# A graph network on one core: edge lists loaded as 128 equal rows, and the first layer's features scaled and split in two parts on two engines ahead of the barrier

## The reference

```python
def _L0_gnn_ref(label, src, dst):
    out_deg = jnp.clip(jax.ops.segment_sum(ones, src, num_segments=n), 1.0)
    in_deg = jnp.clip(jax.ops.segment_sum(ones, dst, num_segments=n), 1.0)
    h = label * (out_deg ** (-0.5))[:, None]
    agg = jax.ops.segment_sum(h[src], dst, num_segments=n)
    return agg * (in_deg ** (-0.5))[:, None]
...
h = jnp.maximum(_layernorm(x, axis=-1), 0.0)
x = x + _L0_gnn_ref(h, src, dst)
h = jnp.maximum(_layernorm(x, axis=-1), 0.0)
x = x + _L1_gnn_ref(h, edge_index, ...)      # two attention layers
h = jnp.maximum(_layernorm(x, axis=-1), 0.0)
x = x + _L2_gnn_ref(h, edge_index, ...)      # attention, rows normalized
h = jnp.maximum(_layernorm(x, axis=-1), 0.0)
x = x + _L3_gnn_ref(h, edge_index, edge_weight1, ...)   # message passing, log_softmax
```

## Time and profile before

| what | value |
|---|---|
| median of 3 runs | 4518.12 us (4517.07 to 4518.27) |
| the profiled execution | 4518.98 us |
| its span | 4516.9 us |
| TensorE busy | 3870.6 us (86%) |
| VectorE busy | 3402.5 us (75%) |
| ScalarE busy | 2879.3 us (64%) |
| GpSimd busy | 516.7 us (11%) |
| mean granted TensorE clock | 0.958 of full speed |

### The profile page before, as it was taken

The page is one execution under the profiler, slowest core; times in us unless marked ns, Lnnn a source line. Parts: engine busy times, 40 slices in busy tenths (PEclk is TensorE's granted clock), DMA queues, the critical chain, the costliest instruction groups (busy, mean ns, idle before and its releaser), DMA issues.

```text
span 4516.9 us, 64954 instructions
## 1 busy us (share of the span) xinstructions
PE 3870.6 (86%) x19132; PEld 2004.2 (44%) x19133; DVE 3402.5 (75%) x5028; ACT 2879.3 (64%) x3229; POOL 516.7 (11%) x1356
## 2 busy tenths in 40 slices
PE   0549999999983998999699999987999998999998
PEld 0546666667651333333333333332333332555555
DVE  4999889889866999996699999879998987211101
ACT  1117677677753999999499999967999997000001
POOL 0005555555510000000000000000000000000000
PEclk9989999999986999999899999998999999999998
DMA  1004344334447454543255444324454541977776
GB/s 45 23 1 149 126 136 156 134 122 155 141 173 93 154 167 151 163 157 114 83 186 165 159 149 160 119 79 157 150 171 151 173 139 54 279 218 239 240 234 188
DMA packets 624622, 660.79 MB, mean 146 GB/s; under 512 B 147489, under 2 KB 590115, under 8 KB 616996
## 3 DMA queue, kind: packets, MB, share of 16 engines
q1 hardware_dynamic: 603898, 524.06, 38.9%
q10 hardware_dynamic: 20524, 134.07, 7.3%
...
## 4 chain that ended last, share of the span: by engine, by line
PE 17%; issue 14%; DVE 8%; DVEq 8%; ACT 5%; DMA 0%; ACTq 0%; SPq 0%
PE psum L1945 12%; DVE sb_arena L1432 5%; ACT sb_arena L2310 4%; DVEq L1435 4%; DVEq L1395 3%; PE psum L1900 2%; DVE sb_arena L1397 2%; ACT psum L2302 1%; PE psum L1991 0%; PE psum L1911 0%; PE psum L1990 0%; DVE sb_arena L1525 0%; PE psum L1974 0%; PE psum L1972 0%; PE psum L1962 0%
## 5 line engine op out<-in xcount | busy, mean ns | idle before, releaser
L1900 PE MATMUL psum<-sb_arena 128*65 128x448 f32 x4116 | 1729.4, 542 | 190.0 <-DVE sb_arena L1432 177.6
L1432 DVE SCALAR_TENSOR_TENSOR sb_arena<-sb_arena 128x896 f32<-128x896 f32 x1029 | 1071.4, 1088 | 206.7 <-ACT sb_arena L2310 189.7
L2302 ACT ACTIVATE psum<-sb_arena,sb_sj 128x896 f32 (+1 forms) x1029 | 1041.0, 1012 | 219.3 <-PE psum L1878 95.9
L2310 ACT ACTIVATE sb_arena<-psum,sb_sj 128x896 f32<-128x896 f32 x1029 | 1019.7, 991 | 96.9 <-PE psum L1911 96.5
L1397 DVE CUSTOM_DVE_ANT_0 sb_arena<-sb_arena 128x6272 uint8<-128x6272 uint8 (+2 forms) x189 | 990.5, 5240 | 74.0 <-DMA sb_arena<-linked 32.7
L1900 PEld LDWEIGHTS psum<-sb_arena 128*65 128x65 f32 x4116 | 557.0, 138 | 881.9 <-issue 501.4
L950 DVE TENSOR_SCALAR sb_arena<-sb_arena 128x392 f16<-128x392 f16 x2352 | 651.1, 344 | 0.0
L1911 PE MATMUL psum<-sb_arena,sb_ones 128*128 128x448 bf16 x2058 | 567.0, 358 | 45.8 <-ACT sb_arena L2279 25.0
L1945 PE MATMUL psum<-sb_arena 128*128 128x448 f16 (+1 forms) x2744 | 544.7, 359 | 33.3 <-DVE sb_arena L1525 22.5
L1687 PE MATMUL psum<-sb_arena 128*128 128x392 f16 x2352 | 476.6, 339 | 38.7 <-DVE sb_arena L950 28.8
L2127 ACT ACTIVATE sb_arena<-psum 128x784 f16<-128x784 f32 x392 | 322.8, 823 | 281.8 <-PE psum L1687 278.7
...
## 6 DMA issues: line engine op xcount, KB each, us to landing
sb_arena<-counts SPq DMA_DIRECT2D x490, 784.0 KB, 6.4
...
sb_arena<-records SPq DMA_DIRECT2D x784, 6.0 KB, 1.7
...
```

The costliest lines, as they stand in the source:

```text
L1432: nc.vector.scalar_tensor_tensor(YE[:, r % RING, :], YE[:, r % RING, :], 1.0, counts_of(g, j), ALU.min, ALU.mult).then_inc(p_ready, 1)
L1900: last = nc.tensor.matmul(psum[0:D + 1, t, 0:HALF], HF[:, r * (D + 1):(r + 1) * (D + 1)], YE[:, r % RING, t * HALF:(t + 1) * HALF], start= ...
L2302: nc.scalar.activation(stage_of(odd, r), of.rearrange("p (t d) -> p t d", t=2), ACT.Relu, bias=sj8[:, r:r + 1], scale=1.0 - SLOPE).then_in ...
L2310: nc.scalar.activation(YE[:, r % RING, :].rearrange("p (t d) -> p t d", t=2), stage_of(odd, r), ACT.Exp, bias=sj2[:, r:r + 1]).then_inc(e_ ...
```

## The change

There are two edits, which share nothing but the preparation.

The first one changes the shapes of the loads. `RUN` is now 1,562, so that 128 equal rows hold 199,936 edges, and the other 64 (`EXTRA`) go one each into one more column of 64 rows. The first numbers of the following rows are loaded as 112 rows, 15 rows and 1 row, behind the edge lists, under a semaphore of their own (`next_in`); the last 64 numbers of `dst` are loaded once more as one row (`extra_i`), and VectorE compares them in one more instruction. The last block of `X` is loaded as 96 rows and 10 rows. The records are written as three pieces instead of two.

The second one moves the work on the first layer's features. The multiplication by the root and the three-way split are cut into two parts (`SPLIT`, 25 and 24 blocks) and now all stand ahead of VectorE's wait for the barrier, while the two copies to bf16 are made by ScalarE, which takes turns with VectorE over `rest_ready` and `piece_kept`. ScalarE, too, now counts up `phase_done` before these copies and waits for the barrier after them. Behind the barrier VectorE only signals `l0_ready`.

```diff
@@ -24,8 +24,10 @@
 TILES = -(-E // (BLK * HT)) * HT
 G = -(-TILES // BLK)
 FULL = TILES // BLK
-RUN = -(-E // BLK)
-LAST_RUN = E - (BLK - 1) * RUN
+RUN = E // BLK
+EXTRA = E - BLK * RUN
+QUEUED = 112
+LAST_ROWS = 96
 KEY = 64
 A0 = 25
 A1 = NB - A0
@@ -35,6 +37,7 @@
 HA = NP // HS
 HB = 28
 HIST_FIRST = 4
+SPLIT = ((0, 25), (25, NB))
 EG = 4
 SUBS = BLK // SUB
 ST = 3
@@ -184,10 +187,11 @@
         blk_i, o = view(o, [BLK, TILES], i32)
         low_i, o = view(o, [BLK, TILES], i32)
         next_i, o = view(o, [BLK, 1], i32)
+        extra_i, o = view(o, [1, EXTRA], i32)
         hist_row, o = view(o, [BLK, 2, TILES], bf16)
         hist_col, o = view(o, [BLK, 2, TILES], bf16)
         ints, _ = view(o, [BLK, 4, TILES], i32)
-        falls_at, _ = view(o, [BLK, RUN], fp32)
+        falls_at, _ = view(o, [BLK, RUN + EXTRA], fp32)
         hot_row, o = view(o, [BLK, 2 * HB // 2, 2 * (HS + SUBS)], bf16)
         hot_col, o = view(o, [BLK, 2 * HB // 2, 2 * (HA + NB)], bf16)
         hot_row = hot_row.rearrange("p (s q) (k t) -> p s q k t", s=2, t=2)
@@ -231,6 +235,7 @@
         pads_set = sem("pads_set")
         dst_in = sem("dst_in")
         src_in = sem("src_in")
+        next_in = sem("next_in")
         ea_in = sem("ea_in")
         consts_ready = sem("consts_ready")
         edges_cast = sem("edges_cast")
@@ -240,6 +245,8 @@
         squared_ready = sem("squared_ready")
         scale_ready = sem("scale_ready")
         scaled = sem("scaled")
+        rest_ready = sem("rest_ready")
+        piece_kept = sem("piece_kept")
         slow_root_in = sem("slow_root_in")
         slow_root_out = sem("slow_root_out")
         x_in = sem("x_in")
@@ -480,12 +487,13 @@
 
             sp.wait_ge(pads_set, 4)
             for flat, to, arrived in ((ap['dst'], dst_i, dst_in), (ap['src'], src_i, src_in), (ap['edge_weight1'].rearrange("e o -> (e o)"), ea_raw, ea_in)):
-                sp.dma_start(to[0:BLK - 1, 0:RUN], flat[0:(BLK - 1) * RUN].rearrange("(p e) -> p e", e=RUN)).then_inc(arrived, 16)
-                sp.dma_start(to[BLK - 1:BLK, 0:LAST_RUN], flat[(BLK - 1) * RUN:E].rearrange("(o e) -> o e", o=1)).then_inc(arrived, 16)
-                if to is dst_i:
-                    sp.dma_start(next_i[0:BLK - 2, :], flat[RUN:(BLK - 1) * RUN].rearrange("(p e) -> p e", e=RUN)[:, 0:1],
-                                 allow_slow_non_contiguous=True).then_inc(arrived, 16)
-                    sp.dma_start(next_i[BLK - 2:BLK - 1, :], flat[(BLK - 1) * RUN:(BLK - 1) * RUN + 1].rearrange("(o e) -> o e", o=1)).then_inc(arrived, 16)
+                sp.dma_start(to[:, 0:RUN], flat[0:BLK * RUN].rearrange("(p e) -> p e", e=RUN)).then_inc(arrived, 16)
+                sp.dma_start(to[0:EXTRA, RUN:RUN + 1], flat[BLK * RUN:E].rearrange("(p o) -> p o", o=1)).then_inc(arrived, 16)
+            firsts = ap['dst'][RUN:BLK * RUN].rearrange("(p e) -> p e", e=RUN)
+            sp.dma_start(next_i[0:QUEUED, :], firsts[0:QUEUED, 0:1], allow_slow_non_contiguous=True).then_inc(next_in, 16)
+            sp.dma_start(next_i[QUEUED:BLK - 1, :], firsts[QUEUED:BLK - 1, 0:1], allow_slow_non_contiguous=True).then_inc(next_in, 16)
+            sp.dma_start(next_i[BLK - 1:BLK, :], ap['dst'][BLK * RUN:BLK * RUN + 1].rearrange("(o e) -> o e", o=1)).then_inc(next_in, 16)
+            sp.dma_start(extra_i[:], ap['dst'][BLK * RUN:E].rearrange("(o e) -> o e", o=1)).then_inc(next_in, 16)
             sp.wait_ge(pads_set, 8)
             for (ki, fo, w, a_both, wn, an, dn) in att:
                 for t in range(BLK // ki):
@@ -506,8 +514,9 @@
                          zero16[:, 0:PACK * 8 // BLK].bitcast(fp32)).then_inc(record_out, 16)
             sp.wait_ge(record_ready, 2)
             sp.dma_start(records[0:BLK * RUN, :].rearrange("(p e) c -> p (e c)", p=BLK), record[:, 0:RUN, :].rearrange("p e c -> p (e c)")).then_inc(record_out, 16)
-            sp.dma_start(records[BLK * RUN:TILES * BLK, :].rearrange("(p e) c -> p (e c)", p=BLK), record[:, RUN:TILES, :].rearrange("p e c -> p (e c)")).then_inc(record_out, 16)
-            sp.wait_ge(record_out, 48)
+            sp.dma_start(records[BLK * RUN:BLK * (RUN + 1), :], record[:, RUN, :]).then_inc(record_out, 16)
+            sp.dma_start(records[BLK * (RUN + 1):TILES * BLK, :].rearrange("(p e) c -> p (e c)", p=BLK), record[:, RUN + 1:TILES, :].rearrange("p e c -> p (e c)")).then_inc(record_out, 16)
+            sp.wait_ge(record_out, 64)
 
             sp.wait_ge(starts_ready, 1)
             sp.dma_start(starts_dram.rearrange("(a j) -> j a", j=SUBS), sub_at[:], allow_slow_non_contiguous=True).then_inc(starts_out, 16)
@@ -628,7 +637,7 @@
         def _(pool):
 
             for to, pad in ((dst_i, NP - 1), (src_i, NP - 1), (ea_raw, 0.0)):
-                nc.gpsimd.memset(to[:, LAST_RUN:TILES], pad).then_inc(pads_set, 1)
+                nc.gpsimd.memset(to[:, RUN:TILES], pad).then_inc(pads_set, 1)
             nc.gpsimd.memset(next_i[:], NP - 1).then_inc(pads_set, 1)
             nc.gpsimd.memset(X[:, NB - 1, :], 0.0).then_inc(pads_set, 1)
             for (_, _, W, _, _, _, _) in att:
@@ -810,7 +819,7 @@
             dve.drain().then_inc(consts_ready, 1)
             nc.vector.memset(misfit[:], 0.0)
             nc.vector.memset(sub_cnt[:], 0.0)
-            dve.wait_ge(dst_in, 64)
+            dve.wait_ge(dst_in, 32)
             nc.vector.tensor_single_scalar(ints[:, 0, :], dst_i[:], 7, ALU.arith_shift_right)
             nc.vector.tensor_single_scalar(ints[:, 1, :], dst_i[:], 3, ALU.arith_shift_right)
             dve.wait_ge(src_in, 32)
@@ -827,11 +836,15 @@
             nc.vector.tensor_copy(hist_row[:, 1, :], ints[:, 1, :])
             nc.vector.scalar_tensor_tensor(record[:, :, 0], dst_i[:], float(KEY), blk_i[:], ALU.mult, ALU.add)
             dve.drain().then_inc(record_ready, 1)
+            nc.vector.memset(falls_at[:, RUN:RUN + EXTRA], 0.0)
+            dve.wait_ge(next_in, 64)
             nc.vector.tensor_tensor(falls_at[:, 0:RUN - 1], dst_i[:, 0:RUN - 1], dst_i[:, 1:RUN], ALU.is_gt)
             nc.vector.tensor_tensor(falls_at[:, RUN - 1:RUN], dst_i[:, RUN - 1:RUN], next_i[:], ALU.is_gt)
             dve.drain()
+            nc.vector.tensor_tensor(falls_at[0:1, RUN:RUN + EXTRA - 1], extra_i[:, 0:EXTRA - 1], extra_i[:, 1:EXTRA], ALU.is_gt)
+            dve.drain()
             nc.vector.tensor_reduce(misfit[:, 0:1], falls_at[:], AX.X, ALU.max)
-            dve.wait_ge(x_in, 32)
+            dve.wait_ge(x_in, 48)
             nc.vector.tensor_reduce(stat[0][:], X[:], AX.X, ALU.add)
             dve.drain()
             nc.vector.tensor_scalar(stat[0][:], stat[0][:], 1.0 / D, None, ALU.mult)
@@ -909,7 +922,17 @@
             dve.wait_ge(scaled, 1)
             nc.vector.tensor_copy(stat[2][:], out_deg[:])
             root(2)
-            nc.vector.tensor_tensor(L_in[:], L_in[:], per_node(stat[1]), ALU.mult)
+            nc.vector.memset(L3p[:, :, D:D + 1], 1.0)
+            for b0, b1 in SPLIT:
+                nc.vector.tensor_tensor(L_in[:, b0:b1], L_in[:, b0:b1], stat[1][:, b0:b1].unsqueeze(2).broadcast_to([BLK, b1 - b0, D]), ALU.mult)
+                dve.drain().then_inc(rest_ready, 1)
+            for k, (b0, b1) in enumerate(SPLIT):
+                dve.wait_ge(piece_kept, k + 1)
+                nc.vector.tensor_tensor(L_in[:, b0:b1], L_in[:, b0:b1], L12[:, b0:b1, 0:D], ALU.subtract)
+                dve.drain().then_inc(rest_ready, 1)
+            for k, (b0, b1) in enumerate(SPLIT):
+                dve.wait_ge(piece_kept, k + 3)
+                nc.vector.tensor_tensor(L3p[:, b0:b1, 0:D], L_in[:, b0:b1], L12[:, b0:b1, D:2 * D], ALU.subtract)
             dve.wait_ge(phase_done, 5)
             dve.drain()
 
@@ -936,8 +959,7 @@
             fast = dve.value_load(starts[0:1, 2 * NWIN:2 * NWIN + 1], min_val=0, max_val=1)
             with dve.If(fast == 1):
 
-                split_features(L_in, L_in, L12, L3p)
-                dve.drain().then_inc(l0_ready, 1)
+                dve.sem_inc(l0_ready, 1)
                 dve.sem_inc(keys_ready, WS)
                 with dve.Fori(0, NH) as h:
                     for k in range(WH):
@@ -2039,7 +2061,8 @@
 
             act.wait_ge(pads_set, 5)
             act.dma_start(X[:, 0:NB - 1, :], ap['x'][0:(NB - 1) * BLK, :].rearrange("(a b) f -> b a f", b=BLK)).then_inc(x_in, 16)
-            act.dma_start(X[0:N - (NB - 1) * BLK, NB - 1, :], ap['x'][(NB - 1) * BLK:N, :]).then_inc(x_in, 16)
+            for b0, b1 in ((0, LAST_ROWS), (LAST_ROWS, N - (NB - 1) * BLK)):
+                act.dma_start(X[b0:b1, NB - 1, :], ap['x'][(NB - 1) * BLK + b0:(NB - 1) * BLK + b1, :]).then_inc(x_in, 16)
             act.wait_ge(ea_in, 32)
             nc.scalar.copy(record[:, :, 2], ea_raw[:])
             act.wait_ge(edges_cast, 1)
@@ -2063,7 +2086,13 @@
                 for t in range(BLK // ki):
                     at = t * (fo + 2) + fo
                     nc.scalar.copy(W[t * ki:(t + 1) * ki, at:at + 2], psum[t * ki:(t + 1) * ki, 5, 2 * l:2 * l + 2])
```

(8 more changed lines are left out.)

## The result

| | before | after |
|---|---|---|
| median | 4518.19 us (4517.07 to 4519.9, 4 runs) | 4463.51 us (4453.28 to 4467.62, 4 runs) |
| the profiled execution | 4518.98 us | 4467.62 us |
| its span | 4516.9 us | 4465.5 us |
| mean granted TensorE clock | 0.958 | 0.957 |

The account below looks back on a forecast made before the run. TensorE, 96% busy in the windows, was taken to set the pace, so an earlier start moves everything. Loads 59.3 plus features 6.8, 66.1 us, off 4518.98 give 4452.9, median 4452.0; own range 4449 to 4457, 8 in 10 4447 to 4461.

Parts of the forecast that it names:

- "VectorE 31.3 us for `dst` and 28.3 us for `src`" go away: Edge-list loads ahead of the histogram: both VectorE waits vanish, 59.6 us, less 0.3 of added work, 59.3 us.
- Slow columns: Rival at the edge-list loads: columns of 4-byte rows issue slowly, 9.2 us per 64 rows, time 4479; chance 0.06.
- one engine: Rival at the edge-list loads: they stay on one engine and their change gives nothing, time 4511; chance 0.03.
- slow casts: Rival at ScalarE's feature casts: they run at 1.94 ns per number, time 4457; chance 0.10.
- Edit 2 gives 6.8 us at ScalarE's first window, by the clearing: Around the barrier: ScalarE's clearing of `stage` decides, and its first window starts at 331.5 instead of 338.32, 6.8 us.
- "Their loads don't move against the barrier": Record loads behind the barrier: unmoved, first pair issued from 322.16 to 323.22 and landing at 324.9.
- "After that SyncE delivers a window's records every 2.1 us (322.16 to 324.24), and TensorE takes some 2.3 (900 us for 388 windows), so records stay ahead": In the windows: SyncE loads one window's records in 2.1 us, TensorE needs 2.3, so records never run short.
- The clock rival: Behind the barrier: denser work lowers TensorE's granted clock, at 0.938 the time is 4542; chance 0.03.
- The range: Whole kernel: forecast's own 4449 to 4457 us, for late lists, the clearing and the run itself.

Follow-up runs that it names:

- e8: Changed kernel with the record loads released early, `AHEAD` 3 instead of 6, and `X` issued only when `src` has landed: 4455.09 us, 0.9855 of the kernel before.
- e10: e8's kernel once more, with no further edit, on the same chip as e9: 4454.36 us, 0.9858 of the kernel before.
- e1: The changed kernel once more, with no edit: 4468.36 us, 0.9890 of the kernel before.
- e2: Kernel before plus the new loads alone, features multiplied and split as before: 4463.30 us, 0.9874 of the kernel before.
- e7: e2's kernel, with SyncE starting its record loads only when the features are split: 4476.76 us, 0.9906 of the kernel before.
- e9: e2's kernel with `AHEAD` 3 instead of 6: 4450.32 us, 0.9858 of the kernel before.
- e3: Kernel before plus the moved features work alone, loads as before: 4517.80 us, 1.0000 of the kernel before.
- e5: Changed kernel with `AHEAD` 3 instead of 6, so fewer windows' keys stand ahead of the self loops: 4456.24 us, 0.9863 of the kernel before.
- e6: Changed kernel with GpSimd's early release of the record loads and `AHEAD` 3 instead of 6: 4456.55 us, 0.9858 of the kernel before.

## Why the prediction was right, and where it was wrong

The terms of the two edits came within 1.8 us. What failed is the step behind them, that the windows keep their old length when they start earlier.

- **"VectorE 31.3 us for `dst` and 28.3 us for `src`" go away**: right. Of the forecast 59.3 us, 57.6 came. The difference is 1.60 us of waits (0.48 and 1.12) and a memset and a compare that take 0.1 to 0.2 us each. The 128 rows of `dst` were in at 5.3 us, where 5.7 was said, and those of `src` at 11.7, where 8.7 was: the queues did take turns, and `src` lost more by it than the 3.0 us for each list allowed. But neither was late for VectorE. What it waited for were the columns of 64 rows, at 10.5 and 13.5, whose landing the prediction put at nothing. Some of that is `X`: with `X` issued later (e8, e10) the columns landed at 5.5 to 6.7 and at 9.0 us and the waits vanish. And some is chance: the same kernel waited 0.24 us in e1.
- **Slow columns, one engine, slow casts**: none happened as described. The first list's column of 64 rows was issued in 0.60 us, so the columns were late in landing and not in issuing; the lists ran on all engines; the casts took 1.53 and 1.47 us, where 1.5 and 1.4 were taken.
- **Edit 2 gives 6.8 us at ScalarE's first window, by the clearing**: right, 6.7. The clearing began 227.5 us behind the histogram's start instead of 224.5, 3.0 us later where some 3.4 were said, and lasted 9.33 us. The features ended 11.2 us after the multiplication began (255.03 to 266.25), where 10.8 was said.
- **"Their loads don't move against the barrier"**: off by 1.4 us against the histogram's start (229.4 us behind it instead of 228.0). GpSimd's line 679, ahead of `rel_ready`, took 1.45 us where the same line took 0.28 before, because VectorE now subtracts beside it. The timeline of before has it as

```profile
320.62 0.28 POOL L670 TENSOR_SCALAR sb_arena<-sb_arena 128x24 f32<-128x24 f32 x1 [0.25 <-issue]
```

  The Trainium skill ("SBUF — State Buffer", "SBUF: two separate sides") says that GpSimd and VectorE share a pair of ports which a VectorE instruction with two inputs in SBUF holds for its whole length against a GpSimd instruction that reads SBUF. The trace agrees: VectorE's subtraction of two such inputs ran from 262.75 to 264.57, and GpSimd's instruction, begun at 263.26, ended at 264.71. In all eight profiles with edit 2 it ended 0.14 us behind VectorE's subtraction and took 0.66 to 1.55 us. In the kernel before and in e2, e7 and e9 it ran beside a cast, which has one input, and took 0.28.
- **"After that SyncE delivers a window's records every 2.1 us (322.16 to 324.24), and TensorE takes some 2.3 (900 us for 388 windows), so records stay ahead"**: this is the step that failed. 2.1 us was one pitch, of the first two windows, and 2.3 was a mean over all halves with the waits between them (392 windows in 924.2 us are 2.36 each). Over 33 windows SyncE takes 2.25 us each (73.9 us before, 74.8 after), and TensorE 2.23 inside the first half. So SyncE doesn't draw ahead by the 0.2 us a window that the prediction counted on, and its 34th window is asked for six windows early, which the prediction didn't ask about at all. The lead of 16.2 us paid for that with 1.1 us to spare; the 8.1 us left after the edit did not. The prediction's own times had this lead in them: 331.5 less 322.16 is 9.3 us, where it had been 16.2. What had been cover for VectorE's split, the time in which SyncE went ahead, was taken away with the split. e2 (lead kept: 924.3), e3 (lead cut without the loads: 934.1), e7 (lead cut and nothing else: 932.4) and e5 (the need for it halved: 923.3) show it from four sides.
- **Why 9.8 us**: at the turn the kernel is 11.2 us later than before (75.2 less 64.0, above). Behind the turn the lower clock was granted for 55.2 us of the windows, against 58.0 before. Half of the 2.8 us less, some 1.4, is an estimate of what that gave back, and 11.2 less 1.4 is 9.8.
- **What of it is the store's**: the 34th window's records took 5.4 us instead of 1.6, so by the arithmetic 3.8 of the 11.2 us are the store's. In e3 they took 2.4 us, 0.8 more than that, and the turn was still at 73.0 us and the hole 6.0: the short lead makes a hole without much help. The store was not moved in any run, so the exact split is argued, not shown.
- **The clock rival**: not this one. The mean granted clock was 0.958 before and 0.957 after. The clock's part in the windows was the 1.4 us above, and in the kernel's favour; before the turn it cost about as much (2.6 us more at the lower level at the start, by half 1.3).
- **The range**: 4449 to 4457 would have held e5, e6, e8, e9 and e10, the kernels without the hole. With it, the profiled execution came out 9.8 us (windows), 1.7 (loads), 0.1 (features) and 3.1 (behind the windows), together 14.7 us above the 4452.9 that had been worked out for it.
